# Two runs of unread products added on TensorE ahead of the second averaging and of the first convolution

## What is computed

```python
x = x + _L0_conv_ref(_gn(x), ...)      # three routed steps
x = x + _L1_conv_ref(_gn(x), ...)      # involution
# in _L0_conv_ref, for each step:
attn = softmax(einsum('nd,bsnd->bns', q, x @ Wk) / sqrt(DIM_HEAD))
pooled = einsum('bns,bsnd->bnd', attn, x @ Wv);  logits = pooled @ Wmlp
weights = softmax(where(allowed > 0.5, logits, -1e9) / ROUTE_TEMP)
wsel = the two largest of weights, made to sum to 1
x_mod = x * (1 + attn_map * scale * softplus(alpha))
y = sum_e wsel[:, e] * conv3x3(x_mod, We[e], be[e])
```

## Time and profile before

| | |
|---|---|
| median of 3 executions | 736.03 us |
| lowest and highest | 734.7 and 736.93 us |
| profiled execution, its own time | 736.84 us |
| its span, first to last instruction | 735.0 us |
| PE busy, of the span | 684.5 us (93%) |
| DVE busy, of the span | 494.2 us (67%) |
| ACT busy, of the span | 276.2 us (38%) |
| POOL busy, of the span | 100.3 us (14%) |
| mean granted clock of TensorE | 0.973 |

### The profile page before, as it was taken

How to read it: one execution, slowest core, us unless ns; L and a number is a source line. 1 busy time by engine, 2 the same in 40 slices (tenths; PEclk the granted TensorE clock), 3 DMA queues, 4 the chain that set the end, 5 groups by cost and what they waited for, 6 DMA issues and landing times.

```text
span 735.0 us, 15059 instructions
## 1 busy us (share of the span) xinstructions
PE 684.5 (93%) x6464; PEld 274.6 (37%) x6464; DVE 494.2 (67%) x764; ACT 276.2 (38%) x364; POOL 100.3 (14%) x57
## 2 busy tenths in 40 slices
PE   6728989999999999999999999997999999999994
PEld 5303433333333333333333333333444444444432
DVE  3686745756644675367449967965877778777781
ACT  3642551312221222132210200004677677676652
POOL 2100000000000000000000110211424234234231
PEclk9968999999999999999999999997999999999997
DMA  7960000000000000000000000000021121121212
GB/s 256 180 120 1 1 1 1 2 1 2 1 1 2 1 2 1 1 2 1 2 1 13 2 2 2 1 1 1 1 58 30 29 58 30 33 54 30 47 41 58
DMA packets 55872, 19.69 MB, mean 27 GB/s; under 512 B 52642, under 2 KB 53636, under 8 KB 55684
## 3 DMA queue, kind: packets, MB, share of 16 engines
q1 hardware_dynamic: 54660, 18.53, 10.8%
q10 hardware_dynamic: 1152, 0.25, 0.2%
HBM read 10.39 MB, written 8.39 MB: 26 GB/s over the span
## 4 chain that ended last, share of the span: by engine, by line
PE 84%; DVE 3%; ACT 2%; issue 1%; POOL 1%; DVEq 0%; POOLq 0%
PE conv L555 49%; PE conv L623 11%; PE att L640 10%; PE att L414 5%; PE att L589 4%; DVE x L1229 2%; PE att L601 2%; PE att L472 1%; PE att L611 1%; PE att L389 1%; ACT x L714 1%; DVE stats L1046 1%; ACT xin L708 0%; POOL x L1295 0%; POOL rstack L1288 0%
## 5 line engine op out<-in xcount | busy, mean ns | idle before, releaser
L555 PE MATMUL conv<-xpad,comb 64*64 64x512 f32 x3456 | 382.6, 592 | 9.5 <-DVE comb L1032 9.5
L555 PEld LDWEIGHTS conv<-xpad,comb 64*64 64x64 f32 x3456 | 129.8, 133 | 232.2 <-issue 226.5
L1229 DVE TENSOR_TENSOR x<-conv,x 128x1024 f32<-128x1024 f32 x144 | 170.2, 1219 | 49.5 <-PE conv L623 49.2
L1032 DVE SCALAR_TENSOR_TENSOR comb<-experts,wsel,comb 128x576 f32<-128x576 f32 x144 | 107.0, 811 | 63.5 <-ACT comb L735 63.5
L623 PE MATMUL conv<-rstack,wse 98*128 98x512 f32 x288 | 101.9, 460 | 5.8 <-POOL rstack L1288 2.6
L745 ACT ACTIVATE x<-conv,bias 128x512 f32<-128x512 f32 x64 | 40.4, 682 | 154.5 <-PE conv L555 154.5
L1021 DVE SCALAR_TENSOR_TENSOR xpad<-att,x 128x1024 f32<-128x1024 f32 x48 | 56.4, 1217 | 38.8 <-PE att L472 38.8
L640 PE MATMUL att<-x,sum_sel 64*32 64x512 f32 x1280 | 79.7, 596 | 0.0
L623 PEld LDWEIGHTS conv<-rstack,wse 98*128 98x128 f32 x288 | 47.9, 193 | 70.9 <-DVE x L1229 34.5
L735 ACT ACTIVATE comb<-experts,wsel 128x576 f32<-128x576 f32 x48 | 34.4, 769 | 82.7 <-PE conv L555 75.3
L1295 POOL TENSOR_TENSOR x<-x,xin 128x1024 f32<-128x1024 f32 x16 | 38.3, 2391 | 131.2 <-ACT x L844 131.2
(11 more groups left out here) (133 smaller groups left out, 403.3 us busy)
## 6 DMA issues: line engine op xcount, KB each, us to landing
x<-in_x SPq DMA_DIRECT2D x32, 256.0 KB, 5.2
out<-comb SPq DMA_DIRECT2D x32, 256.0 KB, 3.1
experts<-in_We SPq DMA_DIRECT2D x2, 576.0 KB
x<-in_c_sum SPq DMA_DIRECT2D x1, 160.0 KB
map_sel<-in_c_map SPq DMA_DIRECT2D x1, 128.0 KB
wr<-in_Wr SPq DMA_DIRECT2D x6, 4.0 KB
x<-in_Ws SPq DMA_DIRECT2D x6, 9.0 KB
ident<-in_c_ident ACTq DMA_DIRECT2D x1, 64.0 KB, 3.9
```

Of the source, the lines that this page charges most:

```text
L555: last = nc.tensor.matmul(conv[own[to], h, HW * rows:HW * rows + HW], comb[own[rows], q % 2, n, t * C:t * C + C], xpad[own[rows], 2 * (q % ...
L1032: v.scalar_tensor_tensor(comb[:, q % 2, n, :], experts[:, e, :], wsel[:, p % 2, j + QP * n, e:e + 1], comb[:, q % 2, n, :], ALU.mult, ALU. ...
L1229: v.tensor_tensor(img(prod[i]), img(conv[:, unit, :]), xip[s][:, kh:kh + H, kw:kw + W], ALU.mult)\
```

## The change

A helper `keep_running(n)` is added to the PE stream. It waits until 7 of the first 8 turns have been copied out of PSUM, that is until half 0 of `conv` is free, and then issues n products of the identity with itself, 128 rows by 128 columns in fp32, into `conv[:, 0, 0:128]`. Nobody reads them. It is called with 6 between `first_attend(0)` and the second averaging, and with 28 between `first_map()` and the first convolution section. The output is unchanged.

```diff
+            def keep_running(n):
+                eng.wait_ge(turn_emptied, GP - 1)
+                for _ in range(n):
+                    nc.tensor.matmul(conv[:, 0, 0:128], ident[:, :], ident[:, :], start=True, stop=True)
...
             first_attend(0)
+            keep_running(6)
             group_average(1, chunk(1), CH, GP)
             first_attend(1)
             logits(0)
             first_map()
+            keep_running(28)
             eng.wait_ge(turn_emptied, GP)
```

## The result

| | before | changed |
|---|---|---|
| median, 13 executions each | 736.14 us | 738.64 us |
| lowest to highest | 734.5 to 738.98 | 737.42 to 740.78 |
| profiled execution, its own time (span) | 736.84 (735.0) | 738.13 (736.2) |
| mean granted clock, profiled execution | 0.973 | 0.978 |

The ratio is 1.0035, with a 95% interval of 1.0019 to 1.0051: the change costs 2.6 us, 1.4 to 3.8 by the interval, a little more than the 0.3% that can be told from no change. The mean clock of TensorE went up, and the time with it.

What follows compares the result with a forecast made beforehand. Bound: one chain without slack from PE's averaging (31.53 us) through DVE's L1009 to PE. 1.4 (Part 1) + 0 (Part 2) on the 736.03 median gives 737.4, taken as 737.3; range 735.4 to 738.9.

Steps and rivals of the forecast that it cites:

- "same": Whole kernel: a measured time of 733.8 to 738.2 us, not distinguishable from no change; chance 0.74.
- Price of a product: One added identity product on PE: taken as 0.235 us, between estimates of 0.225 and 0.26.
- The upper bound: One added product costs at most 0.46 us, read from the first turn, 3.68 / 8, taken as slow throughout.
- rival B: Ahead of the second averaging: loads don't run beside streams, 0.46 us a product, 2.8 for six, time 738.8; chance 0.10.
- Part 1: Six products ahead of the second averaging lie wholly on the chain: 1.4 us later, no gain; bounds 0.4 and 2.8.
- One sign that the prediction gave for being wrong: Second averaging: L401 not moved, where a start about 1.4 us after 31.53 was expected.
- the case that the prediction had priced at 0.4: First attention at full clock: the six products ahead of the averaging fill 1.0 us of real waiting, costing 0.4 us.
- Rival C: The clock falls in the wait ahead of the second attention: scores up to 1.5 us more, time 738.9; chance 0.15.
- Part 2, first step: First convolution section: first taps 1.3 us sooner, taken by PE's wait for L1009, growing from 2.8 to 4.1; value 0.
- Rival D: Ahead of the first convolution: 2.9 us idle follow, so its clock isn't raised; time as forecast; chance 0.62 together with forecast.
- Part 2, last step: PE's restart behind L1009: longer wait doesn't cure the 1.4 us half-clock loss, maybe some tenths worse; 0 added, ±1.4 kept.
- Rival A: The clock pays: kept up at the restart behind L1009, 1.4 us comes back, time 735.0; chance 0.13, half below 735.2.

## Why the prediction was right or wrong

The range of 735.4 to 738.9 held the 738.64, and slower was the sign of its sum. The size was half: +1.3 forecast, +2.5 measured, and the outcome fell just outside the "same" that had 0.74.

- **Price of a product**: right. 0.235 taken, 0.24 measured (six in 1.44 us; 42 in 9.48, 0.226 each). The upper bound was good for half clock: from 46.80 to 48.40 us of the changed kernel, at 0.50, seven records of the 28 products took 1.60 us, 0.46 a product. That the first turn of the earlier trace rows ran at half clock was read from its duration; its granted clock in the trace of before is 1.00. At full clock the loads ran beside the streams, so rival B fell. The rule and the figure of the Trainium skill, "TensorE: Matmul & The Clock Gate", by which a product would be 0.43 (the rule stands in its section "The mechanism", the figure in "LDWEIGHTS (loading the stationary operand)"), do not hold for this full-width fp32 form here.
- **Part 1**: right in place and mechanism; L401 stood directly behind the products in each trace, with no cover where the first attention ran slow (in the first trace of six alone the averaging came 1.46 us later than in before). One sign that the prediction gave for being wrong did occur: L401 had not moved, at 31.23 against 31.53. There the first attention ran at full clock, the case that the prediction had priced at 0.4, and the six cost 0.43. Taken 1.4 (1.3 on the median), measured 1.9 to 2.8 for the six alone. This term was too small, by 0.6 us or more. Of the excess I can name a part only: in both traces of six alone the scores ran slow (averaging to maximum 6.28 and 5.64, 5.11 before), but so they did in kernels without the six.
- **Rival C**: it happened in the changed trace (scores 3.10 instead of 1.92, 1.07 us on the stretch). It is chance in each execution and not an effect that the six were shown to have.
- **Part 2, first step**: right. The wait took the whole gain of the first taps, 4.16 predicted as 4.1, and L1009 did not move by the 28 (27.8 us in every kernel but the one with 16 products ahead of turn(9)).
- **Rival D**: wrong, though it carried the forecast with 0.62. In the changed kernel the wait behind the 28 was 1.16 us and the convolution began at full clock. That the time came near even so is because nothing hangs on that clock, not because the clock stayed low.
- **Part 2, last step**: this is the step that failed. "The longer wait does not cure this and can make the restart some tenths worse; I add 0". The size was left out of the sum; the ±1.4 that the prediction kept in its range covers it. I took the slow restart of the one profiled execution of before for a fixed property. It is not, by the traces of other kernels with nothing added between the scores and turn(9): in executions whose first section runs slow to its third tap PE waits 1.3 to 2.0 us, and in three of those five traces (waits of 1.30, 1.43 and 1.44) the clock held; with the 28 the section was fast and the wait 4.16 in two of three traces. The clock held behind L1009 in three of the seven traces without such products, and in none of the three with the 28. The term should have been up to 1.4, times the share of executions in which the restart would have been fast: with 3 of 7, an estimate of 0.6. The stretches behind turn(9) say about the same, a mean of 43.73 us in those seven and 44.47 in the three. The 28 alone measured 1.5 to 2.4. So the experiments show that this cost hangs on the wait for L1009, since it goes when the wait is shortened or filled; its full size they do not explain.
- **Rival A**: wrong in sign for the same reason. It was dismissed because the wait grows, and that argument should have been carried on to a cost.

The parts do not add: 2.7 and 2.1 us (ratios 1.0036 and 1.0029) for the six, 2.4 and 2.3 for the 28, 2.6 together. That the forecast's range held the sum of two parts that were each too small is in part luck. The intervals, 1.0 to 1.2 us to either side each, leave room for part of that; the rest is open.

## What to carry to other kernels

A product that only keeps an engine's clock up belongs behind the instruction that others wait for, inside a wait that the trace shows, and ahead of work that is on the chain: nine such products one line lower gained 1.5 us where six cost 2.1 to 2.7. Before speeding up work that ends in a wait, ask what the longer wait does to what comes after it; here a start 2.4 us late cost nothing and a fast one 2 us. Where a clock falls in some executions only, one trace shows one case: split the span at the instructions that hang on one another, and compare the stretches over several traces.

## What the runs showed of the hardware

How long PE waited ahead of turn(9), and the clock within the 5 us behind it, in fourteen traces: held after 1.21, 1.30, 1.43, 1.44, 1.79 and 0.83 us and without a wait; fell after 1.87, 1.96, 2.52, 2.58, 2.82, 4.16 and 4.16 us. Those that held are all shorter than those that fell, but these are fourteen executions, and the short waits are also those behind a slow first section or behind added products, so the length of the wait is not shown to be the cause by itself. It is no rule for other places: the wait of 1.95 us near 95 us was followed by a fall in some traces and not in others, and that of 2.66 us ahead of the scores likewise.

A fall need not show in the wait. In the second trace of the 28 alone turn(9) still took 1.09 us, and the clock was 0.50 from 65.6 to 68.9, 1.6 us after PE had restarted. A higher mean clock went with a longer time (0.978 and 738.13 against 0.973 and 736.84), since most of the clock regained lay where PE waited anyway.
